# 128x128 turns as fp32 products with the identity in four column tiles

## The reference

```
x = x + attn_a(layernorm(x))   # causal softmax attention, 16 heads of 16
x = x + ffn(layernorm(x))      # r = sigmoid(xr @ W_r.T); r * (relu(xk @ W_k.T)**2 @ W_v.T)
x = x + attn_b(layernorm(x))   # keys summed with a decay, keys and values normed to length,
                               # scores of each token's next key with the keys up to it
x = x + ffn(layernorm(x))      # xr and xk mix a token with the token before it
```

## Time and profile before

| | |
|---|---|
| runs before | 3199.57, 3200.21, 3204.53 us; median 3200.21 |
| span of the profiled execution | 3194.1 us, first to last instruction |
| what a median run has beyond this span | 6.1 us |
| TensorE matmuls busy | 2905.7 us, 91% |
| TensorE weight loads busy | 1311.1 us, 41% |
| ScalarE, VectorE, GpSimd busy | 2245.2, 1461.8, 845.7 us (70%, 46%, 26%) |
| mean granted TensorE clock | 0.961 of 2.4 GHz |
| transposes at line 872 and 970 | 512 and 128 |

### The profile page before, as it was taken

How to read it: one execution, slowest core, us unless ns; L and a number is a source line. 1 busy time by engine, 2 the same in 40 slices (tenths; PEclk the granted TensorE clock), 3 DMA queues, 4 the chain that set the end, 5 groups by cost and what they waited for, 6 DMA issues and landing times.

```text
span 3194.1 us, 99596 instructions
## 1 busy us (share of the span) xinstructions
PE 2905.7 (91%) x42980; PEld 1311.1 (41%) x42980; DVE 1461.8 (46%) x3534; ACT 2245.2 (70%) x2487; POOL 845.7 (26%) x1278
## 2 busy tenths in 40 slices
PE   6899999999999799997999999999999979999797
PEld 3344334444444344443444444444444434434343
DVE  5322235555455654444344434554555554422434
ACT  2588877777777477773777777777777746777462
POOL 3222223332323232221222222333333312311111
PEclk9899999999999799997999999999999989999898
DMA  4322222222322123222222222222222211222111
GB/s 132 90 78 77 78 60 73 63 75 62 81 67 57 44 63 105 74 70 60 90 80 69 78 90 82 64 70 69 68 63 74 67 52 49 70 64 81 39 52 44
DMA packets 229838, 225.61 MB, mean 71 GB/s; under 512 B 33221, under 2 KB 212933, under 8 KB 229320
## 3 DMA queue, kind: packets, MB, share of 16 engines
q1 hardware_dynamic: 228504, 217.47, 23.8%
q10 hardware_dynamic: 816, 0.79, 0.1%
HBM read 146.80 MB, written 71.32 MB: 68 GB/s over the span
## 4 chain that ended last, share of the span: by engine, by line
PE 71%; DVE 18%; issue 5%; POOL 2%; ACT 2%; SPq 1%; DMA 1%; DVEq 0%; ACTq 0%; POOLq 0%
PE ps L860 44%; PE ps L1067 23%; DVE xn L1153 3%; PE ps L872 3%; DVE pmax L1375 2%; DVE ln_st L1141 2%; ACT probs L816 1%; DVE nw_y L1135 1%; DVE nw_u L1131 1%; DVE nw_u L1133 1%; POOL buf_a L668 1%; POOL probs L719 1%; DVE ln_mv L1147 1%; DVE o_blk L1417 1%; DVE x_buf L1266 1%
## 5 line engine op out<-in xcount | busy, mean ns | idle before, releaser
L816 ACT ACTIVATE probs<-ps 128x1024 f32<-128x1024 f32 x2176 | 2090.6, 1052 | 637.8 <-PE ps L860 635.1
L860 PE MATMUL ps<-q_st,k_st 99*32 99x256 bf16 (+3 forms) x20480 | 1264.6, 350 | 44.0 <-issue 24.9
L1067 PE MATMUL ps<-probs,v_st 128*17 128x512 f32 (+3 forms) x10240 | 1180.7, 536 | 66.2 <-DVE o_blk L1417 30.6
L860 PEld LDWEIGHTS ps<-q_st,k_st 99*32 99x32 bf16 x20480 | 567.3, 96 | 839.7 <-issue 506.6
L719 POOL TENSOR_SCALAR_AFFINE_SELECT probs<-probs 128x256 f32<-128x256 f32 (+1 forms) x896 | 416.8, 483 | 1243.5 <-ACT probs L816 1231.4
L1067 PEld LDWEIGHTS ps<-probs,v_st 128*17 128x17 f32 x10240 | 290.3, 98 | 329.3 <-issue 79.9
L860 PE MATMUL ps<-xT,wT 128*32 128x512 f32 x2048 | 244.9, 594 | 1.3 <-DVE rest L1171 1.3
L1417 DVE STREAM_TRANSPOSE o_blk<-ps 128x512 f32<-128x512 f32 x128 | 90.8, 709 | 326.6 <-PE ps L1067 326.6
L643 POOL TENSOR_TENSOR parts<-rest,parts 128x512 bf16<-128x512 f32 x96 | 120.8, 1258 | 338.9 <-DVE parts L1176 338.9
L1266 DVE TENSOR_TENSOR x_buf<-x_buf,ps 128x512 f32<-128x512 f32 x64 | 44.0, 687 | 270.4 <-PE ps L860 261.1
L872 PE MATMUL ps<-ident,xn 128*128 128x128 f32 x512 | 90.6, 305 | 80.9 <-DVE xn L1153 58.5
(11 more groups left out here) (136 smaller groups left out, 2186.3 us busy)
## 6 DMA issues: line engine op xcount, KB each, us to landing
part_a<-parts SPq DMA_DIRECT2D x192, 128.0 KB
x_buf<-in_L_attn_a_X SPq DMA_DIRECT2D x32, 512.0 KB, 4.6
q_st<-part_a SPq DMA_DIRECT2D x128, 128.0 KB
o_chan<-o_out SPq DMA_DIRECT2D x64, 256.0 KB, 2.4
o_in<-o_chan SPq DMA_DIRECT2D x64, 256.0 KB, 4.5
q_st<-part_b SPq DMA_DIRECT2D x128, 128.0 KB
k_st<-part_a SPq DMA_DIRECT2D x64, 192.0 KB, 3.0
part_b<-parts SPq DMA_DIRECT2D x96, 128.0 KB
```

Of the source, the lines that this page charges most:

```text
L816: nc.scalar.activation(probs[:, g % NP_BUF, :], ps[:, bk:bk + 2, :].rearrange("p a n -> p (a n)"), ACT.Exp, scale=SCALE[ATT[g // (NHG * NG ...
L860: last = pe.matmul(o[c:c + 32], kt[:, c:c + 32], q, **how)
L1067: last = pe.matmul(ps[32 * j:32 * j + VW, bank, q0:q0 + w], v_st[:, k % 2, kb, hg * HG + j, :], p, start=(kb == 0), stop=(kb >= TB * qc), ...
```

## The change

Both turns call the helper `matmul` with the identity as the moving operand, in place of `pe.transpose`. One transpose of 128 columns becomes four products of 32 columns of the same weights with the same 128x128 identity, each to its own 32 partitions of the same output. The product with the identity is computed in fp32.

```diff
             def turn(part, src, kt):
                 free_bank(part)
                 for tb in range(TB):
-                    last = pe.transpose(ps[:, part.bank, tb * P:(tb + 1) * P], src[:, tb, kt * P:(kt + 1) * P], ident[:, :])
+                    last = matmul(ps[:, part.bank, tb * P:(tb + 1) * P], src[:, tb, kt * P:(kt + 1) * P], ident[:, :],
+                                  start=True, stop=True)
                 last.then_inc(s_part, 1)
...
                             for kt in range(KT):
-                                last = pe.transpose(ps[:, part.bank, n * D + kt * P:n * D + (kt + 1) * P],
-                                                    buf_u[:, kt, tb * P:(tb + 1) * P], ident[:, :])
+                                last = matmul(ps[:, part.bank, n * D + kt * P:n * D + (kt + 1) * P],
+                                              buf_u[:, kt, tb * P:(tb + 1) * P], ident[:, :], start=True, stop=True)
                         last.then_inc(s_part, 1)
```

## The result

The changed kernel takes 3234.26 us (median of four runs, 3230.04 to 3246.96), the one before beside it 3200.9: a ratio of 1.0114, 95% interval 1.0093 to 1.0135. It is 33 us slower. The forecast was 35 us faster. Run again later (e12) beside 17 runs of the kernel before, the ratio was 1.0108 (1.0087 to 1.013).

A forecast was written before the change was run, and what follows sets the result against it. TensorE's own instruction stream, busy 91%, was taken as the bound. Savings of 121 x 0.26 + 39 x 0.165 = 37.9 us, less 2.3, took 3194.1 to 3158.5; plus 6.1 gave 3165 us, range 3149 to 3182.

The forecast's parts named there:

- What the new form costs: TensorE's turns: 640 transposes become 2,560 products of 32 columns, 0.109 us per quad, 0.435 per turn.
- Rival A: TensorE's turns: 32-column fp32 loads can't be hidden, quad up to 0.216 us, turn 0.86, to 3228; chance 0.05.
- Rival B: TensorE's turns: a quad's four products stream one behind the other, 0.436 us, turn 1.74, to 3369; chance 0.01.
- The time around a turn: TensorE's turns: about 0.10 us ahead, 0.06 in a slow first step, roughly 0.10 saved behind; ascribed to tiling-mode drains.
- rival E: Around TensorE's turns: the drain comes with semaphores, not the shape; saves 10 us or 0, 3190 to 3200; chance 0.05.
- What is given back: TensorE's 23 waits for GpSimd's mask: each grows by roughly 0.10 us, taking 2.3 us off the saving.
- D: TensorE's waits for rows and output bank absorb half: 18 us go, 3182 is left; chance 0.08.
- C: TensorE's clock: products behind waits keep it up, falls disappear; half gives 3155, all 3145; chance 0.13.
- the sign that was asked for: TensorE's long steady stretch: a granted clock of 1.00 instead of 0.99 would show the clock gaining.

The follow-up runs named there:

- e12: The changed kernel once more, unaltered, beside 17 runs of the kernel before: 3229.28 us, ratio 1.0108.
- e1: The kernel before with all 640 transposes as fp32 products with the identity over the whole array, no column tiles: 3266.53 us, ratio 1.0233.
- e7: The kernel before with line 970 turned as 16-bit halves by tiled bf16 transposes, joined by ScalarE's copy: 3212.62 us, ratio 1.004.
- e2: The kernel before with rows rounded to bf16 and turned as tiled bf16 products at line 872, transposes kept at line 970: 3154.49 us, ratio 0.9884.
- e5: The changed kernel with two column tiles of 64 in its turns in place of four of 32: 3274.86 us, 1.024 of the kernel before.
- e3: The kernel before with rows rounded to bf16 and line 872 turned as bf16 products over the whole array, no column tiles: 3171.66 us, ratio 0.9924.
- e11: A repeat of the kernel with bf16-rounded rows and tiled bf16 products at line 872, beside other kernels: 3156.15 us, 0.9874 of the kernel before.
- e4: The kernel before with each transpose at line 872 issued twice, line 970 as before: 3235.79 us, ratio 1.0134.
- e6: The kernel before with the change at line 970 only, 32 of 160 turns: 3209.54 us, ratio 1.0032.

## Why the prediction was wrong

**The step that failed** is the count under "What the new form costs": "640 transposes [...] become 2,560 products of 32 columns by 128, with as many weight loads", and from it "That is 0.109 us per quad, 0.435 per turn". The pace was right: a group of four costs 0.109 us, after as before. But there are eight groups in a turn and not four, since each fp32 product is two matmuls with two loads. The turn is 0.87 us, and 0.71 - 0.435 saved became 0.16 lost. With 0.87 for 0.435 the prediction's own sum is 121 x 0.16 + 39 x 0.27 + 2.3 = 32 us, to 3232, two from what was measured. No other term is needed for the miss; that the two come so close is in part luck, since the 7 us that the clock gave back and the 5 that nothing accounts for are not in this sum.

**It stood in the rows.** The order of the program, shown with the change, has the values' products as x4 where the trace has x8 (`probs,v_st`, 926.40 in the earlier trace rows), and the scores in bf16 have one matmul for each of the program's. A part of a projection is 16 products in the program (`project_tokens`: two blocks of tokens, two halves of the channels, four pieces), and the row at 1000.11 in the earlier trace rows has it as x32. I read those 32 as "eight quads of 256" products and took from them the price of a quad, 0.216 for 256 columns. A quad of the program costs twice that. A transpose, x4 in both the order and the trace, is not doubled. So one could see before the run that the one form is doubled and the other isn't.

**Rival A had the number, not the reason.** It priced a quad at 0.216 and a turn at 0.86, to 3228 us, and asked for it that 32-column loads can't be hidden. They are hidden: the engine's groups keep 0.109 us, and e1, with loads of 128 columns, costs more, not less. That its 0.216 is nearly the 0.218 of a doubled product is luck. **Rival B** (0.436 per quad) falls with the same rows.

**The rule that I set aside.** The Trainium skill, Perfetto Trace Analysis, "Transposes", wants a logical transpose done as a transpose and not as a standard matmul. I argued against it that a transpose steps no faster than a product of as many columns. For fp32 the rule was right, and the argument compared one instruction with one instruction. For 16-bit values no difference shows: bf16 transposes in e7 and bf16 products in e2 both run at 0.055 us per group of four. What the runs give for 128 columns is 0.109 for the fp32 transpose, 0.218 for the fp32 product and 0.055 for the bf16 product. The Trainium skill, FP8 and Floating Point Precision, "TensorE Precision Notes", counts four passes for true FP32, and 0.218 is four times 0.055. The 4x that the Trainium skill, TensorE: Matmul & The Clock Gate, "Terms", gives the transpose mode for FP32 isn't seen here: it is two.

**The time around a turn (rival E)** was read rightly, and its cause, the change of shape, too. 0.10 ahead is gone with the change (0.44 from the scores), and so are the slow first step and the 0.10 behind. e5 and the pair e2, e3 show that it goes with the tile size, and not with the transposes, the type or the length of a load. The Trainium skill, TensorEngine Tiling (Array Packing), "Key Properties", speaks of a drain where the tiling mode changes. It gives no size, and no row had one, so the prediction's "agree in size with two drains" compared with nothing; e5 puts the price here at 0.10 and 0.15 also between tiles of 64 and of 32 columns. The 0.26 us per busy turn that were forecast were saved, and four more groups at 0.109 cost 0.44.

**What is given back** was right in its place: about 0.1 us at each of 23 waits for the mask was forecast, 3.1 us in 23 came. The other kernels bear it out: these waits are 21.0 to 22.7 us in e12, e11 and e2, which have nothing behind their turns at line 872, and 17.6 to 18.8 in e1, e3, e4 and e6, which keep the 0.10 there, as before with 17.4; only e5, with 20.8, doesn't fit. In the other direction, a saving of 56 us in e2 lost 15 to waits, a quarter. **D**, that half is absorbed, was too much, and its waits (rows) never moved: 58.5, 58.3, and 59.2 in e2.

**C, the clock.** The steady stretch that stood at 0.99 reads 1.00 in the changed kernel, the sign that was asked for:

```profile
1520.00:2590.00 1070.00, 1008.07 (x16872) 501.57 (x16876) 506.09 (x1240) 803.75 (x884) 304.25 (x447) 1.00 0.25 72
```

Over all runs the median time lost to the clock was 125 to 128 us for the kernel before in three sets, 118 and 113 for the changed one, 116 for e4, 122 for e1, 125 for e2 and 131 for e3. So 8 to 15 us came back, but e4 got 8 from transposes alone. The reason given, that products hold the clock where transposes don't, is not borne out. What e4 and the change share is more work in the turn behind the wait; e1 has that too and got a quarter of it, so this stays a guess.

## What to carry over

Count the engine's instructions of a kind in the trace against the program's before giving a new instruction a price: a row's pace per instruction tells nothing until one knows how many of them an operation becomes, and that depends on the type and on the form. To move data through TensorE, transposes or 16-bit products are the cheap forms in these runs; an fp32 product with the identity costs twice an fp32 transpose and four times a bf16 product. A group of another tile size between busy groups of 32 columns costs some 0.25 us around it here (0.21 in bf16), which is worth removing if the new form has no more instructions of that length on the engine than the old.

## What was not expected of the hardware

- An fp32 product is two matmuls and two weight loads, each 0.85 ns a column at full clock with 17, 32 and 64 columns of weights and 0.87 with 128; an fp32 transpose is one.
- Going from tiles of 32 to tiles of 64 columns and back costs as much as going to the whole array and back: 0.10 us ahead, 0.15 inside and behind (fp32).
- 16-bit halves of fp32 values, turned as bf16 transposes in column tiles, run at 0.055 us per group of four with 128 columns; joining them costs ScalarE 1.067 us for 1,024 halves and VectorE 1.224, against 0.601 for the plain ScalarE copy of 512 values.
- The spread between runs of one kernel is mostly the clock: over 17 runs of the kernel before the lost time went from 118 to 138 us and the span with it (correlation 0.86).
